# Forming one of the output projection's weight sums on GpSimd instead of VectorE

## What is computed

```
attn = einsum('bhqk,bkhd->bqhd', probs, v).reshape(B, S, H * DV)      # H = 32 heads, DV = 128
return einsum('bse,ed->bsd', attn, wo)                                # wo is 4096 x 512
```

## Time and profile before

| | |
|---|---|
| median of 3 runs | 1030.31 us (1030.2 to 1031.41) |
| the profiled execution | 1029.89 us, of which the span of the instructions is 1028.1 us |
| TensorE busy | 1020.2 us (99%) |
| VectorE busy | 686.2 us (67%) |
| ScalarE busy | 566.3 us (55%) |
| GpSimd busy | 535.7 us (52%) |
| mean granted TensorE clock | 0.998 |

### The profile page before, as it was taken

How to read it: one execution, slowest core, us unless ns; L and a number is a source line. 1 busy time by engine, 2 the same in 40 slices (tenths; PEclk the granted TensorE clock), 3 DMA queues, 4 the chain that set the end, 5 groups by cost and what they waited for, 6 DMA issues and landing times.

```text
span 1028.1 us, 18453 instructions
## 1 busy us (share of the span) xinstructions
PE 1020.2 (99%) x5504; PEld 877.8 (85%) x5504; DVE 686.2 (67%) x1815; ACT 566.3 (55%) x1503; POOL 535.7 (52%) x477
## 2 busy tenths in 40 slices
PE   8999999999999999999999999999999999999998
PEld 8999888888888888888888888888888788888887
DVE  6778852432466776776776766777697998775571
ACT  4112455545367666767666766766786555543330
POOL 6431378996288778788777797777520000011000
PEclk9999999999999999999999999999999999999999
DMA  9700255762733443444443444334568878850001
GB/s 368 322 0 1 82 194 195 256 260 99 266 88 139 135 148 127 153 153 153 133 134 132 163 141 158 140 115 150 184 235 326 303 252 282 288 187 1 1 31 52
DMA packets 83707, 168.21 MB, mean 164 GB/s; under 512 B 8529, under 2 KB 24913, under 8 KB 82641
## 3 DMA queue, kind: packets, MB, share of 16 engines
q1 hardware_dynamic: 83664, 167.68, 46.8%
HBM read 102.37 MB, written 63.44 MB: 161 GB/s over the span
## 4 chain that ended last, share of the span: by engine, by line
PE 94%; DVE 2%; DMA 1%; POOL 1%; ACT 1%; issue 0%; SPq 0%; POOLq 0%
PE bank L295 28%; PE bank L297 27%; PE bank L296 27%; PE bank L675 4%; PE bank L664 3%; PE bank L693 3%; DMA downT_raw<-down_w 1%; POOL downT_lo L1977 1%; DMA o_raw<-keep_o 1%; PE bank L366 1%; PE bank L469 0%; PE bank L400 0%; PE bank L652 0%; PE bank L303 0%; DVE bank L1359 0%
## 5 line engine op out<-in xcount | busy, mean ns | idle before, releaser
L1594 POOL TENSOR_SCALAR ve<-mv 128x1 f32<-128x1 f32 x24 | 6.3, 264 | 244.4 <-DVE mv L1154 243.8
L860 ACT ACTIVATE bank<-bank,nmax 128x128 f32<-128x128 f32 (+1 forms) x256 | 105.9, 452 | 3.4 <-DVE nmax L1359 3.4
L1372 DVE TENSOR_SCALAR prob<-bank,rinv 128x128 f32<-128x128 f32 (+1 forms) x256 | 95.1, 413 | 4.6
L295 PE MATMUL bank<-xc_lo,wq_hi 128*128 128x512 f32 x224 | 91.7, 409 | 0.0
L1359 DVE CUSTOM_DVE_ANT_0 bank<-bank,mask 128x128 f32<-128x128 f32 (+1 forms) x256 | 83.4, 387 | 11.4 <-PE bank L297 11.4
L744 ACT CAST o_hi<-o_raw 128x1024 fp32r<-128x1024 f32 x56 | 59.3, 1059 | 54.6 <-DMA o_raw<-keep_o 46.4
L295 PE MATMUL bank<-o_lo,ow_hi 128*128 128x512 f32 x224 | 88.9, 397 | 0.5 <-DVE o_lo L1147 0.5
L295 PE MATMUL bank<-xc_lo,wk_hi 128*128 128x512 f32 x224 | 88.6, 396 | 0.0
L297 PE MATMUL bank<-xc_hi,wq_hi 128*128 128x512 f32 x224 | 87.8, 392 | 0.0
L297 PE MATMUL bank<-xc_hi,wk_hi 128*128 128x512 f32 x224 | 87.5, 390 | 0.0
L297 PE MATMUL bank<-o_hi,ow_hi 128*128 128x512 f32 x224 | 87.4, 390 | 0.0
(11 more groups left out here) (202 smaller groups left out, 3140.6 us busy)
## 6 DMA issues: line engine op xcount, KB each, us to landing
o_raw<-keep_o SPq DMA_DIRECT2D x49, 512.0 KB, 4.1
keep_v<-out_hl SPq DMA_DIRECT2D x64, 256.0 KB, 2.3
v<-keep_v SPq DMA_DIRECT2D x64, 256.0 KB, 3.5
keep_o<-att_comb SPq DMA_DIRECT2D x60, 256.0 KB, 2.5
keep_o<-att SPq DMA_DIRECT2D x45, 256.0 KB, 3.0
stage_v<-wv SPq DMA_DIRECT2D x4, 2048.0 KB, 8.6
stage_wq<-wqk SPq DMA_DIRECT2D x16, 512.0 KB, 3.3
keep_vraw<-out_raw SPq DMA_DIRECT2D x64, 128.0 KB, 2.1
```

What stands on the lines that cost most here:

```text
L295: nc.tensor.matmul(dst, a_hi, b_lo, start=first, stop=False, skip_group_check=onto)
L860: nc.scalar.activation(sp[b][:, a:e], sp[b][:, a:e], ACT.Exp, bias=nmax[:, c:c + 1], scale=-1.0, accum_out=rsum[:, c:c + 1]).then_inc(s["e ...
L1372: nc.vector.tensor_scalar(prob[:, b, a:e], sp[b][:, a:e], rinv[:, c:c + 1], None, ALU.mult).then_inc(s["p_ready"], 1)
```

## The change

The four s3 subtractions leave VectorE's program and become four GpSimd instructions of the same size, issued one after the other behind GpSimd's last pair of heads. Each waits for its own quarter of a11 and a21. VectorE's s2 waits for the semaphore `wo_s3_s` as it did before. Nothing else is changed.

```
-        def dve_o_s3(dve, h):
-            for a in ("a11", "a21"):
-                wait_piece(dve, a, h)
-            if h == 0:
-                dve.wait_ge(s["scores_ready"], 8 * PAIRS)
-            nc.vector.tensor_tensor(wo_rows("s3", h), wo_rows("a11", h), wo_rows("a21", h), ALU.subtract).then_inc(s["wo_s3_s"], 1)
-
         def dve_o_s2(dve, h):
             dve.wait_ge(s["wo_s3_s"], h + 1)
             wait_piece(dve, "a22", h)
@@
                 if m in (9, 10, 11, 12):
                     dve_att_sum(dve, m - 9)
-                if m in (13, 15, 17, 20):
-                    dve_o_s3(dve, (13, 15, 17, 20).index(m))
-                elif m in (14, 16, 18, 21):
+                if m in (14, 16, 18, 21):
                     dve_o_s2(dve, (14, 16, 18, 21).index(m))
@@
+        def pool_o_s3(pool, h):
+            for a in ("a11", "a21"):
+                wait_piece(pool, a, h)
+            if h == 0:
+                pool.wait_ge(s["scores_ready"], 8 * PAIRS)
+            nc.gpsimd.tensor_tensor(wo_rows("s3", h), wo_rows("a11", h), wo_rows("a21", h), ALU.subtract).then_inc(s["wo_s3_s"], 1)
@@
             pool_pair(pool, PAIRS - 2, last_w=True)
             pool_pair(pool, LAST, final=True)
+            for h in range(4):
+                pool_o_s3(pool, h)
             for j in range(NT, NT + NT // 2):
                 pool_rstd(pool, j, 0)
```

## The result

The kernel after takes 1033.23 us (1032.76 to 1034.26, 11 runs) against 1030.44 us (1029.17 to 1031.41, 11 runs) for the one before. The ratio is 1.0029, with a 95% interval of 1.0022 to 1.0037: slower by 2.8 us, beyond what can be told from no change. The prediction was 1032.7, within 1030.9 to 1034.2, and slower with a chance of 0.56.

The account below looks back on a forecast made before the run. TensorE was taken as the bound, busy 1020.2 of 1028.1 us, with VectorE nearly second. Terms 0 + 0.5 + 1.3 + 1.3 - 0.75 = +2.35 us on 1030.31 gave 1032.7 us, range 1030.9 to 1034.2.

Parts of the forecast that it names:

- The relief: Four s3 subtractions leave VectorE, 1.14 us each, 4.5 us in all; claimed worth close to nothing on TensorE.
- the wait at step 18: TensorE's 0.64 us stall before projection step 18, held by its `o_lo`; claimed to stay if VectorE merely lost s3.
- A hold: A VectorE instruction kept waiting by a GpSimd subtraction until nearly its end; claimed 2.20 us each.
- the walk: Quarter-by-quarter tally of TensorE's delay in the projection, at 2.72 us a step; claimed +2.35 us in sum.
- quarters 0 and 3: s3 subtractions: first in VectorE's gap before 787.42, cost 0; last delays `o_lo` of step 16, 1.3 us more.
- Quarter 1: Second s3 subtraction, GpSimd 794.25 to 796.65: holds the attention sum of 794.31; TensorE 0.5 us late by step 12.
- Quarter 2: Third s3 subtraction, GpSimd 802.2 to 804.6: VectorE resumes with s2, `o_lo` of step 14 late; TensorE loses 1.3 us.
- the bounds: Limits on the sum: landings moved by 0.35 give 1.8 to 3.2 us; an early second quarter holds step 10's `o_lo`.
- Rival 1 (later turns): VectorE keeps its turn through dense runs, GpSimd enters only where it waits for ScalarE: +1.6, 1031.9 us; chance 0.17.
- Rival 2 (no collision): Subtractions of this size pass each other, GpSimd is free: 1030.3 us, at best 1029.6; chance 0.13.
- Rival 3 (more than the walk): Holds strike two instructions each, or delayed DMA makes token loads late: 1033.5 to 1034.4 us; chance 0.08.
- Rival 4 (the relief counts): VectorE's freed 4.5 us let casts and loads run ahead: 1029.3 us at best; chance 0.02.

## Why the prediction was right

- **The relief is worth nothing**: right as far as the timing tells, that is to within 0.8 us. With s3 left out altogether the time doesn't move. The reason given, that the wait at step 18 stays, did not hold in that kernel's profiled execution, where no wait was left.
- **A hold costs 2.20 us**: right to 0.01. Shown alone where both engines form s3 (+5.05 us, where the walk with s3 kept gives 4.8).
- **It goes through the reading side**: argued before from VectorE's two operands only. Shown now: fills cost nothing, copies and subtractions do.
- **Where the holds strike**: right for quarters 0 and 3, and one instruction early for quarters 1 and 2. Quarter 1 was to strike the attention sum behind `o_lo` of step 10; it struck `o_lo` of step 10 itself, since VectorE was 0.77 us later there (793.94 against 793.17) while the load was 0.1 later. Of this VectorE's delay 0.39 was there before the stretch and the rest came with a late load of step 9. Quarter 2 was to strike s2 of step 14; it struck `o_lo` of step 13.
- **The terms of the sum**: the distances between the same steps before and after give what TensorE lost where. TensorE's timeline, the starts of steps 8 and 10 before, then of step 8 after; the other starts are above and in the earlier trace rows:

```profile
789.88 0.47 PE L295 MATMUL bank<-o_lo,ow_hi 128*128 128x512 f32 x1
...
795.45 0.39 PE L295 MATMUL bank<-o_lo,ow_hi 128*128 128x512 f32 x1
```

```profile
790.28 0.47 PE L295 MATMUL bank<-o_lo,ow_hi 128*128 128x512 f32 x1
```

From step 8 to 10 it is 5.57 us before and 7.23 after, 1.7 lost, where the walk had 0.5 for quarter 1. From 10 to 14 it is 10.88 and 11.35, 0.5 lost, where it had 1.3 for quarter 2. From 14 to 16 it is 5.44 and 6.71, 1.3 lost, as foretold for quarter 3. Behind step 16, 0.8 comes back, against 0.75. The sum is 2.6, as in the stretch (2.58), against 2.35 foretold; by the medians the change is 2.8. So two terms were wrong by 1.2 and 0.8 us in opposite directions. That is no pure luck: the bounds name this variant, with 1 us more at step 10 and most of it back later. But that the middle value came within 0.5 us of the result says little of the single terms.

- **Nothing comes back later**: right, the two later stretches agree to 0.03 us.
- **Rival 1 (later turns)** is out as the rule: of the GpSimd subtractions and copies that found VectorE busy in these runs, all but one got in at the next handover. That one waited 4.6 us and still cost as much. Rival 2 (no collision) is out. Rival 3 (more than the walk) began at 1033.5, close above the measured 1033.23, but what it names isn't there: each GpSimd subtraction held one VectorE instruction, not two, behind 794 us no VectorE row of the stretch waits for a cast, and 0.8 us did come back. Rival 4 (the relief counts) is out, since the change is slower.
- **What the prediction read in the Trainium skill**: the 115 ns stand in "SBUF — State Buffer", section "A bandwidth-pool intuition that's wrong", for a DMA whose descriptors GpSimd couldn't write while a VectorE copy ran. That is not the handover between two instructions, so the 0.14 us here don't contradict them. And the Trainium skill ("Perfetto Trace Analysis", section "Optimizing Scalar/DVE Operations") also says there that the two engines share an SBUF read port and that moving work between them might not help. Rival 2 had less behind it than the prediction says.

What stays open, besides the two groups of times, is what made GpSimd lose four turns at 808.63. It asked 0.03 us before the handover; asking 0.08 to 0.8 before and 0.08 or 0.13 behind never did this, and one that asked 0.01 before found VectorE idle behind. One case isn't enough to say that the moment decides.

## What to carry to other kernels

Moving work from one engine to an idle one pays only if the busy engine's time is what the critical one waits for, and if the two don't share a way to memory: here 4.5 us of relief were worth nothing that the timing shows, and GpSimd's 2.4 us subtractions each held VectorE for 2.2. Before moving, look in the trace for places where the two engines already overlap, and compare durations of equal instructions; two such rows gave the cost to a few hundredths. A hold is harmless where the held engine pauses or is far enough ahead, and cutting it in halves didn't make it cheaper.

## What the runs showed of the hardware

- VectorE subtractions with two operands in SBUF and GpSimd instructions that read SBUF exclude each other for a whole instruction. The hold is the GpSimd instruction's own time less 0.20 us: 2.20 for a subtraction of 128 x 1,024 (2.40), 1.10 for one of 128 x 512 (1.29), 0.84 for a copy of 128 x 1,024 (1.04).
- GpSimd fills of 128 x 1,024 (0.95 us) neither hold nor are held.
- VectorE instructions with one operand in PSUM were not held in the one case where they met a GpSimd subtraction. Where quarters 1 to 3 wait, the last one ran from 819.70 for 2.40 us. VectorE's sums out of PSUM kept their length beside it, and only the `o_lo` behind them, with both operands in SBUF, was held for the rest (2.53 us). GpSimd's timeline, then VectorE's:

```profile
819.70 2.40 POOL L1588 TENSOR_TENSOR wo_s<-wo_raw 128x1024 f32<-128x1024 f32 x1 [6.93 <-DVE o_lo L1147]
```

```profile
819.45 1.27 DVE L1525 TENSOR_TENSOR csum<-bank,os 128x512 f32<-128x512 f32 x2
820.65 2.53 DVE L1147 TENSOR_TENSOR o_lo<-o_raw,o_hi 128x1024 fp32r<-128x1024 f32 x1
```

- The handover lies 0.13 to 0.15 us before the recorded end of the instruction that holds.
- Between two dense streams the turn goes back and forth, one instruction each (the copies and the halves). The exception is the GpSimd subtraction of 6.96 us, which let four VectorE instructions pass.
